# Transposing new token blocks by transfer instead of on TensorE, with re-sequenced engine programs, in a fused attention and feed-forward kernel

## The chip, the cores and the metric

The kernel runs on one core of a Trainium2 chip. The metric is the device time of one execution in microseconds (us). Before the change three executions took 2260.71 to 2260.99 us, with a median of 2260.98 us.

## The reference

The input x has 8 sequences of 1024 tokens with 256 channels, in f32. One block follows the other:

```python
x = x + layernorm(attention(layernorm(x)))
x = x + layernorm(ffn(layernorm(x)))

# attention: 16 heads of width 64, causal, with a bias by clipped distance
q, k, v = einsum('btc,hcd->bhtd', x, Wq), ...
scores = q @ k.T / sqrt(64) + rel_table[clip(rel + 16, 0, 32)]
out = softmax(causal(scores)) @ v            # heads side by side
return out @ Wp + bp

# ffn: x_prev is x shifted by one token
xr, xk = mu_r * x + (1 - mu_r) * x_prev, mu_k * x + (1 - mu_k) * x_prev
return sigmoid(xr @ W_r.T) * (square(relu(xk @ W_k.T)) @ W_v.T)
```

## The kernel before

**Tiling.** The work is cut into 64 units, one for each sequence and pair of heads (8 sequences, 8 pairs). One step n of the main sequence is nearly the same program for all n: it does the attention of unit n, the q, k and v projections of unit n + 2, and the tail (output projection, residual, feed-forward) of one block of 128 tokens. There are 64 blocks, so one step also brings in one new block. Products that need more than f16 are made of f16 high and low parts, with three matmuls for one: high by high, low by high, high by low.

**The new block.** In step n, block g = n + 10 is brought in. SyncE loads its 128x256 f32 rows into `xh` (`load_head`). VectorE takes mean and variance and makes the reciprocal root in eight small operations (`statistics`, `root_step`). GpSimd normalises `xh` in place (`head`, through `normalise`, line 376). TensorE transposes it as two 128x128 f32 transposes into a bank of PSUM called `misc` (`head_transpose`, line 549), ScalarE casts the bank to the f16 high part in the ring `xT` (`head_high`, line 885), and VectorE subtracts that from the bank to give the low part (`head_low`, line 1161). `xT` holds 16 blocks, two sequences. The projections (`project_qk`, line 563, and `project_v`, line 578) read `xT`. The first 8 blocks are made before the main sequence in the same way. There are 56 blocks made inside it, in steps -2 to 53.

**Score tiles.** Unit n has 12 score tiles, S0 to S11, of 512, 384, 256, 128, then five of 512, and 384, 256, 128 keys by queries for each of two heads (`score`, lines 607 and 611). They use two PSUM buffers in turn. S0 of the next unit is made at the end of a step. VectorE adds the bias where there is one (`add_bias`, line 1213), ScalarE exponentiates (`exponential`, line 926) and casts to the f16 high part (`high_probs`, line 944), GpSimd makes the low part (`low_probs`, line 1659; of S0 it is VectorE, line 1181). For S1 to S11 the exponential goes into one of two f32 copies in SBUF, and waits until GpSimd has finished the tile two before it.

**Row maxima.** Nine fills, F0 to F8, of one PSUM buffer (`fill`, lines 629 and 638) give rough scores. VectorE reduces each (`maxima`, lines 1192 and 1197), and TensorE transposes the maxima twice in a step (`transpose_maxima`, line 649, called mt0 and mt1). ScalarE writes the shift (`shift`, line 908), and SyncE spreads it over partitions (`load_shift`).

**Other tasks on TensorE.** q0, q1, k0, k1, v0, v1 are the projections in halves. o0 to o3 weigh the values (`weigh_values`, lines 672 to 674), o2 and o3 a step late. x2t, proj, rk and ffn belong to the tail. All of these write into two banks of `misc`. `TASKS` lists them in their order with a bank for each, and `opened` makes a task wait until the bank's previous task has been read. `project_qk` of q0 waits for `xt_lo`, the low part of the newest block of the ring.

**Order.** Each engine's program is written out by hand as one long list of calls. There is no dynamic scheduling: an instruction that waits holds up everything behind it on its engine. In a step TensorE goes: ffn, S1, F0, q0, o2, S2, S3, F1, o3, F2, q1, S4, F3, S5, k0, mt0, v0, F4, o0, S6, S7, F5, x2t, proj, S8, F6, S9, v1, o1, S10, F7, S11, rk, F8, S0 of the next unit, the head transposes, k1, mt1. Score tiles and fills use 64 rows of the array for each head, all others use 128.

Of the kernel before, what the change touches and what calls it, by code (L numbers as in the profile page):

```python
# [48 lines left out]
TASKS = [("ffn", 1, "ffn"), ("q0", 1, "qkv"), ("o2", 0, "prev"), ("o3", 0, "prev"), ("q1", 1, "qkv"),  # L49
         ("k0", 0, "qkv"), ("v0", 1, "qkv"), ("o0", 0, "att"), ("x2t", 0, "mix"), ("proj", 1, "proj"),  # L50
         ("v1", 0, "qkv"), ("o1", 1, "att"), ("rk", 1, "mix"), ("xt", 1, "xt"), ("k1", 0, "qkv")]
BANK = {name: bank for name, bank, _ in TASKS}
PART = {name: part for name, _, part in TASKS}
NAMES = [name for name, _, _ in TASKS]

# [66 lines left out]
def finished(name, n):  # L122

    return n + {"o2": 0, "o3": 0, "o0": 1, "o1": 1, "mt0": 2, "mt1": 2, "xt": HEAD_LEAD + 1, "proj": 1 - PROJ_LAG, "x2t": 1 - MIX_LAG, "rk": 1 - MIX_LAG,
                "ffn": 1 - FFN_LAG}.get(name, LEAD + 1)
# [17 lines left out]
def build(nc, x, wqkv, wp, bp, table, w_r, w_k, w_v, mu_r, mu_k, out):  # L143
    with ExitStack() as ctx:
# [45 lines left out]
        xh = sb("xh", [P, C], F32)  # L190
        xT = sb("xT", [P, 2, KT, RING], F16)
# [92 lines left out]

        full = {name: sem(f"full_{name}") for name in NAMES + ["mt0", "mt1"]}

        xh_in, xh_ready, xt_hi, xt_lo = sem("xh_in"), sem("xh_ready"), sem("xt_hi"), sem("xt_lo")
        proj_hi, proj_lo, v_hi, v_ready = sem("proj_hi"), sem("proj_lo"), sem("v_hi"), sem("v_ready")
# [52 lines left out]
        def freed(name, n):  # L341

            k = finished(name, n)
            if name[0] == "o" and name[1] in "0123":
                return o_ready[int(name[1])], k
            if name[0] in "qk":
                return proj_lo, 4 * k - 3 + ("q0", "q1", "k0", "k1").index(name) if name != "rk" else k
            if name in ("v0", "v1"):
                return v_ready, 2 * k - 1 + int(name[1])
            if name == "x2t":  # L350
                return mixed_ready, 2 * KT * k
            return {"proj": y_ready, "ffn": z_ready, "xt": xt_lo,
                    "rk": relu_ready}[name], k
# [34 lines left out]
        def _(sp):  # L388
# [92 lines left out]
            for span in ALL_SPANS:  # L481
                def body(m, par, at, has=span.has):
                    n = 2 * m + par
                    if has["xt"] and (not isinstance(m, int) or n > -LEAD):
                        load_head(n + HEAD_LEAD)
                    if has["att"]:
                        load_shift(m, par, 0, 1)
                    if has["next"] and par == 0:
                        load_values(m, par)
                    if has["proj"]:  # L490
                        load_outputs(n, par, at)
                    if has["next"]:
                        load_shift(m, par, 1, 0)
                    if has["proj"]:
                        load_residual(n - PROJ_LAG)
                    if has["next"] and par == 1:
                        load_values(m, par)
                    if has["prev"]:
                        store_chunk(m, par, 1, 1, at)
                    if has["att"]:  # L500
                        store_chunk(m, par, 0, 0, at)
                    if has["ffn"]:
                        store_out(n - FFN_LAG)
                rolled(sp, span, body)
# [23 lines left out]
        def _(pe):  # L528
# [189 lines left out]
            for span in ALL_SPANS:  # L718
                def body(m, par, at, span=span, has=span.has):
# [3 lines left out]
                    if has["ffn"]:  # L723
                        tail_value(n, span)
                    if has["att"]:
                        score(m, par, 0, 1, at)
                    if has["next"]:
# [3 lines left out]
                        fill(m, par, 0, at)  # L731
                    if has["qkv"]:
                        project_qk("q0", n, pair * P, ring, span)
                    if has["prev"]:
                        weigh_values(2, m, par, 1, span)
                    if has["att"]:
                        score(m, par, 0, 2, at)
                        score(m, par, 0, 3, at)
                    if has["next"]:
                        fill(m, par, 1, at)  # L740
                    if has["prev"]:
                        weigh_values(3, m, par, 1, span)
                    if has["next"]:
                        fill(m, par, 2, at)
                    if has["qkv"]:
                        project_qk("q1", n, pair * P, ring, span)
                    if has["att"]:
                        score(m, par, 0, 4, at)
                    if has["next"]:
                        fill(m, par, 3, at)  # L750
                    if has["att"]:
                        score(m, par, 0, 5, at)
                    if has["qkv"]:
                        project_qk("k0", n, pair * P, ring, span)
                    if has["next"]:
                        transpose_maxima(0, n)
                    if has["qkv"]:
                        project_v("v0", n, 4 * par, pair // 2 * 2 * P, ring, span)
                    if has["next"]:
                        fill(m, par, 4, at)  # L760
                    if has["att"]:
                        weigh_values(0, m, par, 0, span)
                        score(m, par, 0, 6, at)
                        score(m, par, 0, 7, at)
                    if has["next"]:
                        fill(m, par, 5, at)
                    if has["mix"]:
# [6 lines left out]
                    if has["att"]:  # L774
                        score(m, par, 0, 8, at)
                    if has["next"]:
                        fill(m, par, 6, at)
                    if has["att"]:
                        score(m, par, 0, 9, at)
                    if has["qkv"]:  # L780
                        project_v("v1", n, 4 * par + 2, pair // 2 * 2 * P, ring, span)
                    if has["att"]:
                        weigh_values(1, m, par, 0, span)
                        score(m, par, 0, 10, at)
                    if has["next"]:
                        fill(m, par, 7, at)
                    if has["att"]:
                        score(m, par, 0, 11, at)
                    if has["mix"]:
                        tail_gate_and_key(n, span)  # L790
# [3 lines left out]
                    if has["xt"]:  # L794
                        head_transpose(n, span)
                    if has["qkv"]:
                        project_qk("k1", n, pair * P, ring, span)
# [40 lines left out]
            tail_value(N, LAST)  # L838
            weigh_values(2, N // 2, 0, 1, LAST)
            weigh_values(3, N // 2, 0, 1, LAST)  # L840
            for j in range(NB):
# [32 lines left out]
        def _(act):  # L874
# [104 lines left out]
            for span in ALL_SPANS:  # L979
                def body(m, par, at, has=span.has):  # L980
# [6 lines left out]
                    if has["att"]:  # L987
                        exponential(m, par, 0, 1)
                        high_probs(m, par, 0, 1)
                    if has["qkv"]:  # L990
                        high_part("q0", m, par, at)
                    if has["att"]:
                        exponential(m, par, 0, 2)
                        high_probs(m, par, 0, 2)
                        exponential(m, par, 0, 3)
                    if has["qkv"]:
                        high_part("q1", m, par, at)
                    if has["att"]:
                        exponential(m, par, 0, 4)
                        high_probs(m, par, 0, 3)  # L1000
                        high_probs(m, par, 0, 4)
                    if has["qkv"]:
                        high_part("k0", m, par, at)
                    if has["next"]:
                        shift(m, par, 1, 0)
                    if has["att"]:
                        exponential(m, par, 0, 5)
                    if has["prev"]:
                        high_outputs(1, m, par, 1)
                    if has["qkv"]:  # L1010
                        values_high("v0", m, par)
                    if has["att"]:
                        high_probs(m, par, 0, 5)
                        exponential(m, par, 0, 6)
                    if has["mix"]:
                        tail_tokens(n)
                    if has["att"]:
                        high_probs(m, par, 0, 6)
                        exponential(m, par, 0, 7)
                        high_probs(m, par, 0, 7)  # L1020
                        exponential(m, par, 0, 8)
                        high_probs(m, par, 0, 8)
                        exponential(m, par, 0, 9)
                        high_probs(m, par, 0, 9)
                    if has["qkv"]:
                        values_high("v1", m, par)
                    if has["att"]:
                        exponential(m, par, 0, 10)
                        high_outputs(0, m, par, 0)
                    if has["mix"]:  # L1030
                        tail_gate(n)
                    if has["att"]:
                        high_probs(m, par, 0, 10)
                    if has["xt"]:
                        col = (m + HEAD_LEAD // 2) % (RING // P // 2) * 2 * P
                        col = (col if isinstance(m, int) else act.snap(col)) + par * P
                        head_high(n + HEAD_LEAD, col, misc[BANK["xt"]])
                    if has["att"]:
                        exponential(m, par, 0, 11)
                    if has["qkv"]:  # L1040
                        high_part("k1", m, par, at)
                    if has["next"]:
                        shift(m, par, 1, 1)
                        exponential(m, par, 1, 0)
                    if has["att"]:
# [754 lines left out]
```

## Time and profile before

| what | value |
|---|---|
| time, median of 3 | 2260.98 us |
| profiled execution, its own time | 2259.63 us |
| span of its instructions | 2257.8 us |
| TensorE matmul busy | 2133.1 us (94%) |
| VectorE busy | 1953.9 us (87%) |
| ScalarE busy | 1679.4 us (74%) |
| GpSimd busy | 1645.2 us (73%) |
| mean granted TensorE clock | 0.991 |
| chain that ended last | PE 86%, DVE 5%, ACT 3% |
| DMA queue of the kernel, share of 16 engines | 24.1% |

Busy time is summed over the whole span, the start and the end of the program included. The matmul ends are modelled. The chain that ended last is followed back from the last instruction to whatever released each step, and names where the time went. The profiled execution is 1.35 us shorter than the median.

### The profile page before, as it was taken

Reading aid. Unit: us, or ns where it says so; the run is one execution under the profiler, and the core shown is the slowest. Engines: PE = TensorE matmul, PEld = TensorE weight load, DVE = VectorE, ACT = ScalarE, POOL = GpSimd, SP = SyncE. Lnnn points to the kernel's source line nnn. Section 1 sums busy time; section 2 is a strip of 40 time slices with the busy share of each in tenths; the row PEclk is TensorE's granted clock in tenths of the full one; section 3 lists DMA queues with packets and bytes.
Section 4 is the critical chain, followed back from the end, with each engine's and each line's share of the span. In section 5 each row is a group of like instructions: output and inputs, shape, how many; then the busy total and the mean of one; then the engine's idle time right before and its main releaser. Section 6 shows DMA issues by size and latency. Waiting matters only on the chain.

```text
span 2257.8 us, 74896 instructions
## 1 busy us (share of the span) xinstructions
PE 2133.1 (94%) x29568; PEld 1456.7 (65%) x29568; DVE 1953.9 (87%) x5265; ACT 1679.4 (74%) x2526; POOL 1645.2 (73%) x1314
## 2 busy tenths in 40 slices
PE   3787899999999999999999999999999999999975
PEld 1354556676666767666666766666676667666664
DVE  6776778999999999999999999999999998888856
ACT  2576877787778777877877787787778778777733
POOL 1365766787778778777877877787787777777851
PEclk9999999999999999999999999999999999999998
DMA  7011012222321232232122223212322321222250
GB/s 176 23 39 44 28 37 60 68 60 61 72 61 49 63 71 62 58 73 67 42 63 73 62 56 72 70 44 58 72 62 57 73 67 49 48 66 65 58 125 22
DMA packets 306319, 139.77 MB, mean 62 GB/s; under 512 B 142512, under 2 KB 305200, under 8 KB 305968
## 3 DMA queue, kind: packets, MB, share of 16 engines
q1 hardware_dynamic: 305968, 134.98, 24.1%
q8 instruction: 234, 3.83, 0.7%
q14 instruction: 117, 0.96, 0.1%
HBM read 24.25 MB, written 43.06 MB: 30 GB/s over the span
## 4 chain that ended last, share of the span: by engine, by line
PE 86%; DVE 5%; ACT 3%; issue 2%; POOL 2%; DMA 1%; DVEq 0%; POOLq 0%; ACTq 0%; SPq 0%
PE score_ps L607 17%; PE misc L563 15%; PE misc L578 7%; PE misc L680 7%; PE misc L672 6%; PE max_ps L629 6%; PE misc L673 6%; PE misc L674 6%; PE score_ps L611 5%; PE misc L700 3%; PE misc L703 2%; PE max_ps L638 2%; PE misc L711 2%; POOL probs L1659 1%; ACT probs_f L926 1%
## 5 line engine op out<-in xcount | busy, mean ns | idle before, releaser
L1659 POOL TENSOR_TENSOR probs<-probs_f,probs 128x1024 f16<-128x1024 f32 (+3 forms) x704 | 1119.3, 1602 | 402.1 <-ACT probs L944 395.1
L926 ACT ACTIVATE probs_f<-score_ps,score_unit 128x1024 f32<-128x1024 f32 (+3 forms) x704 | 618.1, 878 | 271.4 <-DVE score_ps L1213 215.0
L1197 DVE TENSOR_REDUCE row_max<-max_ps 128x2 f32<-128x1024 f32 (+2 forms) x640 | 633.8, 1007 | 55.7 <-PE max_ps L638 53.7
L944 ACT CAST probs<-probs_f 128x1024 f16<-128x1024 f32 (+3 forms) x704 | 563.5, 810 | 10.5
L672 PE MATMUL misc<-v_pair,probs 128*128 128x65 f16 x4608 | 443.8, 193 | 2.2 <-DVE o_norm L1225 2.1
L673 PE MATMUL misc<-v_pair,probs 128*128 128x64 f16 x4608 | 442.8, 193 | 0.0
L674 PE MATMUL misc<-v_pair,probs 128*128 128x65 f16 x4608 | 441.7, 193 | 0.0
L672 PEld LDWEIGHTS misc<-v_pair,probs 128*128 128x128 f16 x4608 | 416.7, 97 | 23.3 <-issue 4.0
L673 PEld LDWEIGHTS misc<-v_pair,probs 128*128 128x128 f16 x4608 | 418.1, 97 | 8.0
L674 PEld LDWEIGHTS misc<-v_pair,probs 128*128 128x128 f16 x4608 | 418.3, 97 | 0.0
L563 PE MATMUL misc<-xT,w_split 128*128 128x512 f16 x1536 | 383.2, 386 | 10.7 <-DVE w_split L1316 6.7
L607 PE MATMUL score_ps<-q_hi,k_hi 64*128 64x512 f16 (+3 forms) x1536 | 254.9, 329 | 27.6 <-ACT probs_f L926 20.1
L1213 DVE TENSOR_TENSOR score_ps<-score_ps,bandT 128x288 f32<-128x288 f32 (+2 forms) x576 | 243.6, 423 | 25.3 <-PE score_ps L611 23.9
L563 PEld LDWEIGHTS misc<-xT,w_split 128*128 128x128 f16 x1536 | 135.5, 99 | 179.8 <-issue 50.5
L611 PE MATMUL score_ps<-shift_all,shift_unit 64*128 64x512 f16 (+3 forms) x1536 | 250.8, 323 | 0.0
L607 PE MATMUL score_ps<-q_lo,k_hi 64*128 64x512 f16 (+3 forms) x1536 | 250.7, 323 | 0.0
L607 PE MATMUL score_ps<-q_hi,k_lo 64*128 64x512 f16 (+3 forms) x1536 | 250.7, 323 | 0.0
L629 PE MATMUL max_ps<-k_hi,q_hi 64*128 64x512 f16 (+3 forms) x1536 | 221.7, 326 | 23.6 <-DVE row_max L1197 15.0
L578 PE MATMUL misc<-w_split,xT 128*128 128x256 f16 x1536 | 189.6, 273 | 0.0
L578 PEld LDWEIGHTS misc<-w_split,xT 128*128 128x128 f16 x1536 | 145.5, 98 | 40.6 <-issue 20.3
L680 PE MATMUL misc<-wp_split,oT 128*128 128x256 f16 x1344 | 157.1, 274 | 0.0
L607 PEld LDWEIGHTS score_ps<-q_hi,k_hi 64*128 64x128 f16 x1536 | 74.6, 93 | 115.3 <-issue 49.4
(168 smaller groups left out, 3715.2 us busy)
## 6 DMA issues: line engine op xcount, KB each, us to landing
v_pair<-v_calc SPq DMA_DIRECT2D x64, 516.0 KB, 4.0
o_scratch<-o_stage SPq DMA_DIRECT2D x128, 256.0 KB, 2.5
xh<-x SPq DMA_DIRECT2D x56, 128.0 KB, 2.5
x_res<-x SPq DMA_DIRECT2D x56, 128.0 KB, 2.1
out<-out_sb SPq DMA_DIRECT2D x56, 128.0 KB, 2.4
shift_all<-shift_row SPq DMA_DIRECT2D x256, 1.0 KB
probs<-wqkv SPq DMA_DIRECT2D x1, 3072.0 KB, 13.4
probs<-band_scratch SPq DMA_DIRECT2D x8, 144.0 KB, 3.8
```

Of the source, the lines that this page charges most:

```text
L563: last = pe.matmul(bank[:], w_split[:, w, which, k, bass.ds(pair, P)], xT[:, a, k, bass.ds(ring + half * 512, 512)], start=step == 0, stop ...
L578: last = pe.matmul(bank[:, i * 2 * P:(i + 1) * 2 * P], xT[:, a, k, bass.ds(ring + (first + i) * P, P)], w_split[:, w, 2, k, bass.ds(pairs, ...
L607: pe.matmul(tile[:, h, 0:width], k_part[rows, ring, keys], q_part[rows, ring, cols], start=step == 0, stop=False)
L611: last = pe.matmul(tile[:, h, 0:width], shift_unit[rows, :], shift_all[side][rows, cols], start=False, stop=True)
L629: last = pe.matmul(max_ps[:, h, col:col + width], qk_hi[0][rows, ring, i * P:(i + 1) * P], qk_hi[1][rows, ring, key:key + width], start=Tr ...
L672: pe.matmul(bank[:, at:at + D + 1], high, v_high, start=j == 0, stop=False)
L673: pe.matmul(bank[:, at:at + D], high, v_low, start=False, stop=False)
L674: last = pe.matmul(bank[:, at:at + D + 1], low, v_high, start=False, stop=j == i)
L926: nc.scalar.activation(dst, score_ps[t % 2][:, :, 0:width], ACT.Exp, scale=score_unit[:]).then_inc(exp_done, 1)
L944: nc.scalar.copy(dst, src).then_inc(hi_done, 1)
L1197: last = dve.tensor_reduce(dst[:, :, i % 4:i % 4 + 1], max_ps[:, :, col:col + width], AX.X, ALU.max)
L1659: pool.tensor_tensor(low, copy_of(par + ahead, t)[:, 0:2 * width], high, ALU.subtract).then_inc(lo_done_pool, 1)
```

## The change

The new block no longer goes through TensorE and PSUM. GpSimd normalises `xh` as before. ScalarE casts `xh` to f16 into half of a new buffer `x_parts` (`head_parts`), GpSimd subtracts to fill the other half (`head_low`), and SyncE issues one transposing transfer from `x_parts` into the ring (`transpose_head`). q0 waits for that transfer.

```diff
+        x_parts = sb("x_parts", [P, 2, C], F16)
...
             def load_head(g):
-                held(full["xt"], g)
+                held(x_lo, g - NB)
                 sp.dma_start(xh[:], x_rows[g]).then_inc(xh_in, 16)
+
+            def transpose_head(n):
+                g = n + HEAD_LEAD
+                held(x_lo, g - NB + 1)
+                held(full[LAST_PROJECTION], n + LEAD)
+                col = g % (RING // P) * P
+                sp.dma_start_transpose(xT[:].rearrange("p a k t -> p (a k) t")[:, :, col:col + P],
+                                       x_parts[:].rearrange("p a c -> p (a c)")).then_inc(xT_in, 16)
...
-            def head_transpose(n, span):
-                pe.wait_ge(xh_ready, n + LEAD + 1)
-                bank = opened("xt", n, span)
-                for k in range(KT):
-                    last = pe.transpose(bank[:, k * P:(k + 1) * P], xh[:, k * P:(k + 1) * P], ident[:])
-                last.then_inc(full["xt"], 1)
...
                 if name == "q0":
-                    pe.wait_ge(xt_lo, n + HEAD_LEAD if span.has["xt"] else G)
+                    pe.wait_ge(xt_lo, NB)
+                    wait(pe, xT_in, 16 * min(n + LEAD, G - NB))
...
+            def head_parts(n):
+                k = n + LEAD
+                act.wait_ge(xh_ready, k + 1)
+                wait(act, xT_in, 16 * k)
+                nc.scalar.copy(x_parts[:, 0, :], xh[:]).then_inc(x_hi, 1)
...
-                normalise(pool, "xh", xh[:], xh[:], k, (full["xt"], 0))
+                normalise(pool, "xh", xh[:], xh[:], k, (x_hi, 0))
+
+            def head_low(n):
+                pool.wait_ge(x_hi, n + LEAD + 1)
+                pool.tensor_tensor(x_parts[:, 1, :], xh[:], x_parts[:, 0, :], ALU.subtract).then_inc(x_lo, 1)
```

`head_high` and `head_low` of the old kind stay for the first 8 blocks alone.

All engines get new orders in the main sequence, and `TASKS` new banks to match:

- TensorE: S1, F0, o2, o3, S2, F1, S3, q0, ffn, F2, S4, S5, F3, o0, q1, v0, mt0, S6, F4, S7, o1, S8, F5, k0, k1, F6, v1, S9, S10, F7, x2t, proj, S11, F8, S0 of the next unit, rk, mt1.
- ScalarE (E exponential, H high part, by tile): E1, H1, E2, high parts of the previous second output half, q0, H2, E3, H3, E4, H4, E5, H5, shift for mt0, q1, E6, v0, H6, E7, H7, k0, E8, k1, H8, v1, high parts of the first output half, copy after x2t, E9, H9, E10, E11, H10, H11, shift for mt1, three gate operations after rk, E0 and H0 of the next unit, `head_parts`.
- GpSimd: low parts of tiles 1 to 4, low parts of the second output half of the previous unit, tiles 5 to 7, the residual normalisation, tiles 8 and 9, low parts of the first output half, tiles 10 and 11, `head`, `final` (two operations), `head_low`, `residual` (two operations).
- SyncE: shift for the columns of S4 to S11, `load_head`, values, shift for the next unit, outputs (a transposing transfer of four times the size), residual, store of outputs, values, store of outputs, store of the result, `transpose_head`.
- VectorE: `gated` and the outputs 2 and 3 change places, roots and maxima are spread anew, and the old `head_low` is gone. The operations are otherwise the same.

## Rows read from the trace of the kernel before

**Rows 1.** Windows view: busy time of each engine in two stretches.

```profile
60.00:352.00 292.00, 249.90 (x3542) 152.41 (x3543) 218.53 (x428) 211.16 (x301) 172.10 (x116) 0.98 0.15 39
352.00:1857.00 1505.00, 1503.46 (x21208) 1038.75 (x21206) 1383.12 (x3830) 1185.44 (x1787) 1199.61 (x958) 1.00 0.25 62
```

**Rows 2.** Timeline of TensorE, end of a step (start, duration, instruction).

```profile
1449.19 0.39 PE L629 MATMUL max_ps<-k_hi,q_hi 64*128 64x512 f16 x2
...
1449.51 0.38 PE L607 MATMUL score_ps<-q_hi,k_hi 64*128 64x512 f16 x2
...
1450.47 0.44 PE L549 MATMUL misc<-ident,xh 128*128 128x128 f32 x2
1450.74 1.46 PE L563 MATMUL misc<-xT,w_split 128*128 128x512 f16 x6
...
1452.15 1.03 PE L711 MATMUL misc<-wv_sb,k_act 128*128 128x256 f32 x4
```

**Rows 3.** Timeline of TensorE, the beginning of a step.

```profile
1420.29 0.34 PE L607 MATMUL score_ps<-q_hi,k_hi 64*128 64x384 f16 x2
...
1421.36 1.47 PE L563 MATMUL misc<-xT,w_split 128*128 128x512 f16 x6
1422.66 0.19 PE L672 MATMUL misc<-v_pair,probs 128*128 128x65 f16 x1
...
1424.74 0.28 PE L607 MATMUL score_ps<-q_hi,k_hi 64*128 64x256 f16 x2
...
1425.83 0.20 PE L672 MATMUL misc<-v_pair,probs 128*128 128x65 f16 x1
...
1428.64 0.39 PE L629 MATMUL max_ps<-k_hi,q_hi 64*128 64x128 f16 x4
...
1429.06 1.47 PE L563 MATMUL misc<-xT,w_split 128*128 128x512 f16 x6
1430.46 0.39 PE L607 MATMUL score_ps<-q_hi,k_hi 64*128 64x512 f16 x2
```

**Rows 4.** Timeline of TensorE, tail tasks of one step.

```profile
1438.65 0.44 PE L693 MATMUL misc<-ident,y 128*128 128x128 f32 x2
...
1441.64 0.39 PE L607 MATMUL score_ps<-q_hi,k_hi 64*128 64x512 f16 x2
...
1447.23 1.13 PE L700 MATMUL misc<-wr_sb,mixed 128*128 128x256 f32 x4
```

**Rows 5.** Timeline of ScalarE in the same step.

```profile
1439.12 0.37 ACT L958 COPY x2T<-misc 128x256 f32<-128x256 f32 x1 [0.23 <-PE misc L693]
...
1445.32 0.90 ACT L926 ACTIVATE probs_f<-score_ps,score_unit 128x768 f32<-128x768 f32 x1
1446.25 0.83 ACT L944 CAST probs<-probs_f 128x768 f16<-128x768 f32 x1
...
1449.29 0.39 ACT L965 ACTIVATE gate<-misc 128x256 f32<-128x256 f32 x1 [0.38 <-PE misc L703]
...
1450.31 0.60 ACT L944 CAST probs<-probs_f 128x512 f16<-128x512 f32 x1
```

**Rows 6.** Timeline of GpSimd in the same step.

```profile
1422.36 2.28 POOL L1665 TENSOR_TENSOR o_stage<-o_norm,o_stage 128x512 f16<-128x512 f32 x2
...
1433.03 0.67 POOL L1659 TENSOR_TENSOR probs<-probs_f,probs 128x256 f16<-128x256 f32 x1 [3.65 <-ACT probs L944]
...
1448.80 1.64 POOL L1659 TENSOR_TENSOR probs<-probs_f,probs 128x768 f16<-128x768 f32 x1
1451.45 1.22 POOL L376 TENSOR_SCALAR out_sb<-z,z_mv,z_r 128x256 f32<-128x256 f32 x1 [1.01 <-DVE z_r L1143]
1452.76 0.72 POOL L1692 TENSOR_TENSOR out_sb<-x,out_sb 128x256 f32<-128x256 f32 x1
```

**Rows 7.** SyncE's timeline, and the DMA view of that issue (us to landing).

```profile
1427.62 2.33 SPq L429 DMA_TRANSPOSE oT<-o_scratch  x1
...
oT<-o_scratch SPq DMA_TRANSPOSE x1, 4.4
```

More of the change, by code:

```diff
@@ L54 @@
 NAMES = [name for name, _, _ in TASKS]
+LAST_PROJECTION = [name for name in NAMES if name in ("q0", "q1", "k0", "k1", "v0", "v1")][-1]
 WP_SPLIT = 5
@@ L122, in finished @@
 def finished(name, n):
-    return n + {"o2": 0, "o3": 0, "o0": 1, "o1": 1, "mt0": 2, "mt1": 2, "xt": HEAD_LEAD + 1, "proj": 1 - PROJ_LAG, "x2t": 1 - MIX_LAG, "rk": 1 - MIX_LAG,
+    return n + {"o2": 0, "o3": 0, "o0": 1, "o1": 1, "mt0": 2, "mt1": 2, "proj": 1 - PROJ_LAG, "x2t": 1 - MIX_LAG, "rk": 1 - MIX_LAG,
                 "ffn": 1 - FFN_LAG}.get(name, LEAD + 1)
@@ L283, in build @@
             sem("x0_in"), sem("x0_stats"), sem("x0_aggr"), sem("x0_root"), sem("x0_ready"))
-        full = {name: sem(f"full_{name}") for name in NAMES + ["mt0", "mt1"]}
+        full = {name: sem(f"full_{name}") for name in NAMES + ["xt", "mt0", "mt1"]}
         xh_in, xh_ready, xt_hi, xt_lo = sem("xh_in"), sem("xh_ready"), sem("xt_hi"), sem("xt_lo")
+        x_hi, x_lo, xT_in = sem("x_hi"), sem("x_lo"), sem("xT_in")
         proj_hi, proj_lo, v_hi, v_ready = sem("proj_hi"), sem("proj_lo"), sem("v_hi"), sem("v_ready")
@@ L483, in body @@
                     n = 2 * m + par
+                    if has["att"]:
+                        load_shift(m, par, 0, 1)
                     if has["xt"] and (not isinstance(m, int) or n > -LEAD):
                         load_head(n + HEAD_LEAD)
-                    if has["att"]:
-                        load_shift(m, par, 0, 1)
                     if has["next"] and par == 0:
                         load_values(m, par)
-                    if has["proj"]:
-                        load_outputs(n, par, at)
                     if has["next"]:
@@ L503, in body @@
                         store_out(n - FFN_LAG)
+                    if has["xt"]:
+                        transpose_head(n)
                 rolled(sp, span, body)
@@ L731, in body @@
                         fill(m, par, 0, at)
+                    if has["prev"]:
+                        weigh_values(2, m, par, 1, span)
+                        weigh_values(3, m, par, 1, span)
+                    if has["att"]:
+                        score(m, par, 0, 2, at)
+                    if has["next"]:
+                        fill(m, par, 1, at)
+                    if has["att"]:
+                        score(m, par, 0, 3, at)
                     if has["qkv"]:
                         project_qk("q0", n, pair * P, ring, span)
[L734 to L742, printed above, removed]
+                    if has["ffn"]:
+                        tail_value(n, span)
                     if has["next"]:
                         fill(m, par, 2, at)
-                    if has["qkv"]:
-                        project_qk("q1", n, pair * P, ring, span)
                     if has["att"]:
                         score(m, par, 0, 4, at)
+                        score(m, par, 0, 5, at)
                     if has["next"]:
@@ L761, in body @@
                     if has["att"]:
-                        weigh_values(0, m, par, 0, span)
-                        score(m, par, 0, 6, at)
                         score(m, par, 0, 7, at)
+                        weigh_values(1, m, par, 0, span)
+                        score(m, par, 0, 8, at)
                     if has["next"]:
                         fill(m, par, 5, at)
+                    if has["qkv"]:
+                        project_qk("k0", n, pair * P, ring, span)
+                        project_qk("k1", n, pair * P, ring, span)
+                    if has["next"]:
+                        fill(m, par, 6, at)
+                    if has["qkv"]:
+                        project_v("v1", n, 4 * par + 2, pair // 2 * 2 * P, ring, span)
+                    if has["att"]:
+                        score(m, par, 0, 9, at)
+                        score(m, par, 0, 10, at)
+                    if has["next"]:
+                        fill(m, par, 7, at)
                     if has["mix"]:
@@ L793, in body @@
                         score(m, par, 1, 0, at)
[L794 to L797, printed above, removed]
+                    if has["mix"]:
+                        tail_gate_and_key(n, span)
                     if has["next"]:
@@ L989, in body @@
                         high_probs(m, par, 0, 1)
+                        exponential(m, par, 0, 2)
+                    if has["prev"]:
+                        high_outputs(1, m, par, 1)
                     if has["qkv"]:
@@ L992, in body @@
                     if has["att"]:
-                        exponential(m, par, 0, 2)
                         high_probs(m, par, 0, 2)
                         exponential(m, par, 0, 3)
+                        high_probs(m, par, 0, 3)
+                        exponential(m, par, 0, 4)
+                        high_probs(m, par, 0, 4)
+                        exponential(m, par, 0, 5)
+                        high_probs(m, par, 0, 5)
+                    if has["next"]:
+                        shift(m, par, 1, 0)
                     if has["qkv"]:
@@ L998, in body @@
                     if has["att"]:
[L999 to L1009, printed above, removed]
+                        exponential(m, par, 0, 6)
                     if has["qkv"]:
                         values_high("v0", m, par)
[L1012 to L1016, printed above, removed]
                     if has["att"]:
@@ L1479, in body @@
+                    if has["qkv"]:
+                        low_part("k1", m, par, at)
+                        values_low("v1", m, par)
+                    if has["att"]:
+                        add_bias(m, par, 0, 9, at)
+                    if has["next"]:
+                        maxima(m, par, 1, 7)
+                    if has["att"]:
+                        add_bias(m, par, 0, 10, at)
                     if has["mix"]:
                         mix(n)
+                    if has["att"]:
+                        add_bias(m, par, 0, 11, at)
@@ L1481, in body @@
+                    if has["next"]:
+                        maxima(m, par, 1, 8)
+                    if has["proj"]:
+                        projected(n)
+                    if has["next"]:
+                        join_maxima(m, par, 1)
+                    if has["proj"]:
+                        statistics("y", y, n - PROJ_LAG, y_ready, n - PROJ_LAG + 1)
                     if has["ffn"]:
                         root_step("z", n - FFN_LAG, 4)
-                    if has["xt"]:
-                        root_step("xh", n + LEAD, 4)
@@ L1537, in body @@
                     if has["proj"]:
+                        root_step("y", n - PROJ_LAG, 3)
+                    if has["ffn"]:
+                        root_step("z", n - FFN_LAG, 5)
+                    if has["proj"]:
+                        root_step("y", n - PROJ_LAG, 4)
+                    if has["ffn"]:
+                        root_step("z", n - FFN_LAG, 6)
+                    if has["proj"]:
+                        root_step("y", n - PROJ_LAG, 5)
                         root_step("y", n - PROJ_LAG, 6)
-                    if has["qkv"]:
-                        low_part("k1", m, par, at)
+                    if has["ffn"]:
+                        root_step("z", n - FFN_LAG, 7)
                     if has["proj"]:
@@ L1723, in body @@
                         low_probs(m, par, 0, 4)
-                    if has["mix"]:
-                        residual_norm(n, par)
+                    if has["prev"]:
+                        low_outputs(1, m, par, 1)
                     if has["att"]:
```

236 lines of the change are left out of this document (95 added, 141 removed).

## The prediction, made before the result was known

> **What bounds the kernel now.** First the windows view: in the stretch of full steps, 352 to 1857 us, TensorE is busy 1503.46 of 1505 us, at full clock, while VectorE has 92%, ScalarE 79% and GpSimd 80% [rows 1]. The reader should see that no other engine costs anything there: TensorE's own issue time is the whole time. The stretch holds 46 steps, so a step takes 1505 / 46 = 32.72 us. From 60 to 352 us it is busy only 249.9 of 292 us [rows 1]. There the steps have no tail work yet, and other engines hold it up in places. Second, TensorE's timeline, where the distance from one start to the next is what a task really costs (durations overlap) [rows 2 to 4]. Third, the timelines of ScalarE, GpSimd and SyncE, for the new chain that the change makes [rows 5 to 7].
>
> **What goes from TensorE.** The two head transposes start at 1450.47, and k1 at 1450.74: 0.27 us a step [rows 2]. Behind them goes VectorE's subtraction, hidden today by TensorE's saturation, worth nothing as long as TensorE bounds. ScalarE's cast keeps its size.
>
> **What the new order on TensorE saves.** Each change between tasks on 64 rows and on 128 rows costs time. A fill inside a 64-row group takes 1449.51 - 1449.19 = 0.32 us [rows 2], and a fill between 128-row tasks takes 0.42 (1428.64 to 1429.06) [rows 3], so 0.10 going to 128 rows. A projection followed by 128-row work takes 1.30 (1421.36 to 1422.66), followed by a score tile 1.40 (1429.06 to 1430.46) [rows 3], so 0.10 going back. The old step has nine 64-row groups, the new one eight (S1 F0; S2 F1 S3; F2 S4 S5 F3; S6 F4 S7; S8 F5; F6; S9 S10 F7; S11 F8 S0). That saves 0.20 us a step. In steps without tail work the counts are equal. So with nothing late, a full step is 0.27 + 0.20 = 0.47 us shorter.
>
> **What the change adds: a wait at q0.** In step n, q0 waits for the transfer issued by the program of step n - 1, though its data is needed at most once in eight steps. I lay both sides out from the start of S1.
>
> q0's place on TensorE: S1, F0 and the change to 128 rows 1.07; o2 2.08 - 0.10 = 1.98, as o3 follows it; o3 with the change back 2.81; S2, F1, S3 with a change 1.09 (the same three in the old order, 1424.74 to 1425.83) [rows 3]. Together 6.95 us.
>
> The transfer's chain starts at x2t of the step before. From there to S1: x2t and proj 2.99 [rows 4]; S11, a quarter of a 512 tile, where S0 with its change is 0.96, so 0.22; F8 and S0 with a change 1.28 [rows 2]; rk, 1447.23 to 1449.19, 1.96 less the change 0.10, so 1.86 [rows 2, 4]; mt1 0.11 (k1 and mt1 take 1.41 together, k1 1.30) and a change 0.10 [rows 2, 3]. Sum 6.56, so x2t starts at -6.56. ScalarE copies it 0.47 later (1438.65 to 1439.12), and can start E9 about 0.27 after that; H9 starts 0.93 after E9 and lasts 0.83 [rows 4, 5]. GpSimd can start tile 9 at -4.03. From there it works without a gap: tile 9 1.64, output low parts 2.28 / 2 = 1.14, tile 10 about 1.12 and tile 11 0.67, `head` about 1.2, the first half of `final` 1.31 up to its second half, which lasts 0.72, then `head_low` about 0.67, as the low part of a tile with 256 elements [rows 6]. Sum 8.5, so `head_low` ends at 4.45 and SyncE issues at about 4.55. ScalarE's side must end by 3.8 and does so within 0.3: shift about 0.3, gate operations 1.02, E0 and H0 at most 4/3 of 0.90 and 0.83, the copy 0.4, about 4 us in all [rows 5].
>
> The landing is not in the trace. The nearest row is the transposing transfer of outputs: four times the size, issued in 2.33 us, landed at 4.4 [rows 7]. If issue time goes with size, the new one is issued in 0.58 and lands at 4.4 - 1.75 = 2.65. From below I take 2.0, as if only the part of that time outside the issue counted (4.4 - 2.33 = 2.07); from above 4.4, if a transfer of any size costs what this one does. I take 2.65, as both are the same kind of instruction. Then q0 may start at 4.55 + 2.65 = 7.2 and finds its place at 6.95: a wait of 0.25, and with 0.1 us for the semaphores 0.35 us a step. Nothing makes this up, as all later work on TensorE moves with q0 and the chain hangs on x2t of the same step. At 2.07 there is no wait, at 4.4 it is 2.1 us.
>
> The Trainium skill, in "DMA: Bandwidth & Descriptors" (section on the anatomy of one DMA), gives a fixed 2.0 us plus bytes over 436 GB/s, for a GpSimd-issued transfer. An estimate from it for 128 KB is 2.3 us, which would make the wait about 0.1 and a full step 0.4 us shorter. The larger transfer would take 3.2 by that rule, and the trace has 4.4 [rows 7], so the rule does not agree there.
>
> **What else moves.** SyncE: the next `load_shift` now stands behind the store of the result and `transpose_head`. It is issued at about 4.55 + 0.6 and could land by 8.5, and S4 starts at 9.6. Cover 1 us; a full-size issue of 2.33 would use it up. VectorE: 30.1 us of work in a step of 32.3, less the subtraction, is the tightest engine [rows 1]. Going through its list beside TensorE's, the near places are q1's low part before o1 (about 0.4 us), k0's before v1 (0.3) and v1's before proj (0.3). I cost them at nothing; one late by 0.3 would cost 0.3 a step. GpSimd gets 0.67 us a step and goes from 26.1 to 26.8 of 32.3 [rows 1, 6].
>
> **The sum.** Full steps with a new block: 45 x (0.35 - 0.47) = -5.4. Eight more without one: 8 x -0.20 = -1.6. Steps before 352 us: TensorE idles 42 us there [rows 1], part of it at set-up that stays. The old order runs tiles 5 to 8 back to back against GpSimd's pace, and the new one spreads them. I put 1 us a step for 8 steps, after paying the same wait, so -8, with bounds of -16 and +8. Set-up and end: nothing, within 3 us. Together -15: 2259.63 - 15 = 2244.6 for the profiled execution's own time, and 1.35 more against the median: **2246 us**. This kernel's measurement can tell about 0.2% (4.5 us) from no change.
>
> **The rivals.**
> - *The transfer is hidden* (landing 2.1 or less, or GpSimd earlier than I add up). The wait is 0: 45 x -0.47 = -21, with the rest -10: 2229. For it: the 4.4 us of the large one includes an issue that a small one may not need. Against: 0.35 us would have to go from a chain whose terms are nearly all measured, or from the landing. Chance 0.24.
> - *The wait grows to a new bound, slower* (the other side). A transfer read from SBUF in pieces costs more to issue than one from DRAM. From a landing of 3.0 the wait is 0.7, the steps' loss 45 x 0.23 = 10 eats the gain elsewhere, and beyond it the time is above before. At 4.4: 45 x (2.1 - 0.47) = 73, and the early steps pay as well: 2335. Its middle is a landing of 3.5, wait 1.2, +33 and little from the early steps: 2290. For it: the store of the result is in the queue 0.6 us ahead, and all 16 engines' packets must land. Against: the clean row at 4.4 for four times the bytes. Chance 0.22. The Trainium skill, same page (section on why a DMA increments its semaphore by 16), describes SBUF-to-SBUF transposes on earlier generations as one push command per tile, and has a lower price for a DRAM source; no transpose from SBUF is in this trace.
> - *VectorE's handoffs come late.* With the forecast's wait and 0.3 us more: +13 on the forecast, 2260, no change. For it: 92% busy with in-order waits. Against: q0's wait gives VectorE room. Chance 0.12.
> - *The change doesn't do what it says*: the transposes stay elsewhere on TensorE. The diff leaves none. Chance 0.
>
> **How the numbers follow.** The forecast has 0.42, and its own range is 2238 to 2256. The rivals have 0.24, 0.22 and 0.12. Faster by over 0.2% takes the forecast, the hidden case: 0.66 less 0.03 for the forecast's upper end, so 0.63. Within 0.2%: the VectorE case and that end, 0.13. Slower: 0.24. The range goes from 2226, just under the hidden case, to 2282, which leaves the worse half of the slow case out.
>
> **What would show it.** TensorE has no L549 row, and eight 64-row groups. q0's L563 waits for the DMA xT once in each step, with a mean near 0.35. The transfer's row has an issue near 0.6 and a landing near 2.65. `head_low` ends about 4.5 us after S1. A full step is near 32.6 us. I am wrong if q0 waits over 0.7, or if TensorE waits elsewhere in each step, for VectorE's `q_lo`, `k_lo` or `row_max`.

## The result, and the profile after

| | before | after |
|---|---|---|
| median of the runs | 2260.98 us | 2325.01 us (2322.42 to 2329.78, 4 runs) |
| ratio, 95% interval | 1 | 1.0282 [1.0268, 1.0295] |
| span of the profiled execution | 2257.8 us | 2320.6 us |

The change makes the kernel 64 us slower (2325.01 - 2260.98). The prediction was 2246 us, faster, with a range up to 2282; the result lies outside it.

The windows view of after, with the stretches of [rows 1] (from:to and length, then busy us and count of TensorE's matmuls, its weight loads, VectorE, ScalarE and GpSimd, the granted clock, the DMA engines' busy share and GB/s):

```profile
60.00:352.00 292.00, 245.02 (x3486) 149.08 (x3486) 210.47 (x411) 207.62 (x296) 176.84 (x123) 0.95 0.15 41
352.00:1857.00 1505.00, 1441.92 (x20308) 983.88 (x20309) 1325.91 (x3638) 1147.84 (x1723) 1179.94 (x966) 0.99 0.27 64
```

TensorE was busy for 1503.46 of 1505 us before [rows 1] and is for 1441.92 now: it idles 63 us, and no other engine does more than before. The waits view of TensorE, from 352 to 1857 us (line, what it waited for: us in total, times, longest):

```profile
PE misc L569 <- issue: 61.0, 43, 2.7
PE max_ps L655 <- DVE row_max L1207: 0.9, 1, 0.9
PE score_ps L613 <- ACT probs_f L933: 0.6, 2, 0.3
PE misc L569 <- DMA xT<-x_parts: 0.5, 1, 0.5
```

Nearly all the idle time, 61.5 of 63 us, stands before one line, L569, the projections from the ring (L563 before), once in each of 44 steps. The view says "issue" for 43 of them. The timeline says what it was. TensorE, from S1 to the task behind q0 (start, duration, instruction, idle time before it):

```profile
1427.56 0.34 PE L613 MATMUL score_ps<-q_hi,k_hi 64*128 64x384 f16 x2
...
1428.63 0.20 PE L678 MATMUL misc<-v_pair,probs 128*128 128x65 f16 x1
...
1433.42 0.28 PE L613 MATMUL score_ps<-q_hi,k_hi 64*128 64x256 f16 x2
...
1434.36 0.22 PE L617 MATMUL score_ps<-shift_all,shift_unit 64*128 64x128 f16 x2
...
1435.38 1.46 PE L569 MATMUL misc<-xT,w_split 128*128 128x512 f16 x6 [0.81 <-issue]
1436.67 1.03 PE L717 MATMUL misc<-wv_sb,k_act 128*128 128x256 f32 x4
```

SyncE in the same step, and the tile view's row of the transfer (duration of the issue: min/median/max in ns):

```profile
1432.19 0.34 SPq L455 DMA_DIRECT2D out<-out_sb  x1
1432.85 1.24 SPq L450 DMA_TRANSPOSE xT<-x_parts  x1
1434.19 1.29 SPq L402 DMA_DIRECT2D shift_all<-shift_row  x2
...
L450 SPq DMA_TRANSPOSE xT<-x_parts x56: 1203/1238/2421, 55.1 to 1914.6; - x56
```

q0 was ready at 1435.38 - 0.81 = 1434.57, 7.01 us after S1. The transfer is issued at 1432.85, 5.29 us after S1, and lands 2.4 us later, at about 1435.25; q0 starts about 0.1 us after that. In a later step the transfer takes 4.1 us, lands at about 1499.65 + 4.1 = 1503.75, and q0 starts at 1503.88, again about 0.1 us behind it:

```profile
1499.65 1.22 SPq L450 DMA_TRANSPOSE xT<-x_parts  x1
```

```profile
1503.88 2.44 PE L569 MATMUL misc<-xT,w_split 128*128 128x512 f16 x6 [2.50 <-issue]
1506.11 1.77 PE L717 MATMUL misc<-wv_sb,k_act 128*128 128x256 f32 x4
```

So the wait is for the landing, whatever the view calls it. The second pair of rows shows one thing more. From q0 to the ffn task takes 1506.11 - 1503.88 = 2.23 us, where it took 1436.67 - 1435.38 = 1.29 in the other step. The windows view over another such step (a wait of 2.0 us, then q0 at 449.4), and over the step with the short wait:

```profile
449.40:453.40 4.00, 3.95 (x12) 2.00 (x12) 0.13 (x1) 1.19 (x3) 0.01 (x1) 0.57 0.11 33
...
1435.00:1439.00 4.00, 3.62 (x28) 2.03 (x30) 2.77 (x6) 2.65 (x6) 2.27 (x2) 1.00 0.50 144
```

The granted clock is 0.57 on average behind the long wait and 1.00 behind the short one: the engine ran mostly at 1.2 GHz, the lower level, where otherwise it has 2.4. That costs another 1.7 us in such a step: the step with the wait of 2.50 us takes 36.53 us, where one with a wait of 0.81 takes 33.18, and of the 3.35 us between them the longer wait is 1.69.

The length of each step, from the start of the exponential of S0 to the next one on ScalarE's timeline, gives an account that all the runs below share. In the tables, steps 9 to 53 are the 45 with tail work and a new block, steps 54 to 61 have tail work and no new block (step 54 still waits at q0, for the last one).

### The profile page after: what moved, and what is told of

The parts are those of the page before. It is cut to its first block and busy times, and to the rows that moved or that the text cites. A ratio compares the mean times of both kernels' runs of the same rounds, so it can differ in the third digit from the quotient of the medians.

```text
span 2320.6 us, 74837 instructions
## 1 busy us (share of the span) xinstructions
PE 2125.9 (92%) x29456; PEld 1438.6 (62%) x29456; DVE 1945.4 (84%) x5209; ACT 1684.9 (73%) x2526; POOL 1681.5 (72%) x1370
## 5 line engine op out<-in xcount | busy, mean ns | idle before, releaser
L569 PE MATMUL misc<-xT,w_split 128*128 128x512 f16 x1536 | 374.0, 387 | 84.5 <-issue 71.8
L678 PE MATMUL misc<-v_pair,probs 128*128 128x65 f16 x4608 | 438.4, 194 | 0.6 <-issue 0.6
L679 PE MATMUL misc<-v_pair,probs 128*128 128x64 f16 x4608 | 436.7, 193 | 0.0
L680 PE MATMUL misc<-v_pair,probs 128*128 128x65 f16 x4608 | 435.8, 193 | 0.0
L569 PEld LDWEIGHTS misc<-xT,w_split 128*128 128x128 f16 x1536 | 137.8, 99 | 242.0 <-issue 102.5
L881 ACT CAST q_hi<-misc 128x512 f16<-128x512 f32 x128 | 73.1, 571 | 108.4 <-PE misc L569 108.4
```

The lines of the kernel that those rows point to most:

```text
L569: last = pe.matmul(bank[:], w_split[:, w, which, k, bass.ds(pair, P)], xT[:, a, k, bass.ds(ring + half * 512, 512)], start=step == 0, stop ...
L678: pe.matmul(bank[:, at:at + D + 1], high, v_high, start=j == 0, stop=False)
L679: pe.matmul(bank[:, at:at + D], high, v_low, start=False, stop=False)
L680: last = pe.matmul(bank[:, at:at + D + 1], low, v_high, start=False, stop=j == i)
```

## The experiments

**What was asked.** The theory: q0 waits for the landing, which is both issued later and takes longer than forecast, and the rest of the new order gives what it should. The rivals: the new order itself costs time, VectorE's handoffs are late, or the idle time has nothing to do with the slower clock. Four kernels were run first, and e5_roots and e6_warm after their results. The kernel before was run again beside each group (2261.9 us beside the first four, 2264.06 beside the last two), and the ratios are to these.

### e1_relax: q0 waits for a transfer of an earlier step

```diff
-                    wait(pe, xT_in, 16 * min(n + LEAD, G - NB))
+                    wait(pe, xT_in, 16 * ((n + LEAD) // NB * NB))
```

The wait is then for what q0 really reads, and only once in NB steps for the transfer just issued. Everything else stays.

> q0 waits for the new block only where the projections first read it, in one step of eight; the transfer, its chain and every engine's order stay. If the wait at q0 is what made the changed kernel slow, it is left in 7 of 56 steps, a full step takes 32.35 us as the steps without a new block do, and the time falls from 2325 by about 70 to about 2253 us. If the new orders on VectorE, ScalarE or GpSimd are the true limit, another wait takes its place on TensorE in each step, and the time stays above 2290.

Measured: 2251.03 us, ratio 0.9958 to before [0.9943, 0.9972]. TensorE's waits from 376 to 1930 us:

```profile
PE misc L569 <- issue: 8.4, 6, 2.7
PE score_ps L613 <- DMA shift_all<-shift_row: 2.2, 7, 0.5
```

One wait's threshold holds 74 us of the time, the slower clock included, and turns the change from slower to faster, by 0.4%. The second row is a cover of the prediction that was used up: S4 waits for the shift that stands behind the transposing transfer in SyncE's queue, in 7 steps, by 2.2 us in all.

### e2_early: the same wait, the transfer issued earlier

The edit puts `head_low` ahead of `final` on GpSimd, `head_parts` ahead of E0's cast on ScalarE, and the transfer ahead of the store on SyncE.

```diff
@@ GpSimd
                         head(n)
+                        head_low(n)
                     if has["ffn"]:
                         final(n, par)
-                    if has["xt"]:
-                        head_low(n)
@@ ScalarE
-                        high_probs(m, par, 1, 0)
                     if has["xt"]:
                         head_parts(n)
+                    if has["next"]:
+                        high_probs(m, par, 1, 0)
@@ SyncE
-                    if has["ffn"]:
-                        store_out(n - FFN_LAG)
                     if has["xt"]:
                         transpose_head(n)
+                    if has["ffn"]:
+                        store_out(n - FFN_LAG)
```

> The wait at q0 stays in every step, but the chain before it is shortened: GpSimd makes the low part before the final normalisation, ScalarE makes the high part before the cast of S0, SyncE issues the transfer before the store of the result. The issue should move from 5.3 to about 3.7 us after S1. With landings of 2.4 to 4.3 us the wait should then be 0 in most steps and at most 1.1, and the time about 2257. If landing gets longer because the transfer now meets other work, or GpSimd's delayed low parts hold up the exponentials, it stays above 2290.

Measured: 2253.53 us (8 runs), ratio 0.9963 [0.9952, 0.9974]. The transfer goes out 3.64 us after S1 instead of 5.29. What is left of the waits, from 352 to 1857 us, and GpSimd's wait for ScalarE's copy, which keeps the issue from coming earlier still:

```profile
PE misc L569 <- issue: 10.2, 15, 1.2
```

```profile
1421.02 0.68 POOL L1672 TENSOR_TENSOR x_parts<-xh,x_parts 128x256 f16<-128x256 f32 x1 [1.00 <-ACT x_parts L893]
```

The wait can go either way: by asking for less, or by having the data sooner. The remaining 15 waits are those of the 15 longest landings, 3.5 to 4.5 us.

### e3_both: e1 and e2 together

> Both edits. With the wait theory nothing is left to wait for at q0, so the time is that of full steps of 32.35 us: about 2247 us, below the kernel before (2261). A rival, that the reordered GpSimd costs more than the wait did in the one step of eight, puts it above the run with the relaxed wait alone.

Measured: 2238.62 us (2236.16 to 2241.2), ratio 0.9902 [0.9887, 0.9917]: faster than both kernels, 22 us below before and 86 below after. The windows view of the full steps:

```profile
400.00:1800.00 1400.00, 1398.67 (x19863) 960.48 (x19859) 1301.50 (x3586) 1117.93 (x1688) 1159.66 (x950) 1.00 0.28 67
```

TensorE is full again (1398.67 of 1400 us). With 1.3 us of waits left at q0 in two steps, the new order shows what it gives. The step lengths (us, sums over steps; a full step is 32.82 before with a new block):

| steps | before | after | e1_relax | e2_early | e3_both | e4_later | e5_roots | e6_warm |
|---|---|---|---|---|---|---|---|---|
| 1 to 8 | 259.5 | 266.2 | 262.1 | 266.2 | 262.2 | 266.6 | 265.3 | 266.2 |
| 9 to 53 | 1476.5 | 1533.9 | 1468.8 | 1465.1 | 1456.2 | 1568.1 | 1513.0 | 1525.4 |

In e3_both nearly every step of the second row has 32.34 us (45 x 32.34 = 1455.3). The 1476.5 of before less 1456.2 is 20.3, or 0.45 us a step, against the 0.47 of the prediction. The forecast of 2247 for this kernel was 8 us too high: its steps of 32.35 us came, and it does not say what it took for the rest.

### e4_later: the same transfer, issued behind the next shift

```diff
                         load_shift(m, par, 0, 1)
+                    if runs("xt", n - 1):
+                        transpose_head(n - 1)
...
-                    if has["xt"]:
-                        transpose_head(n)
```

> The transfer is issued behind the next shift's two transfers, 1.3 us later; nothing else moves. If only the wait counts, each of some 54 steps loses 1.3 us and the time is about 2395. If the granted clock also falls after each wait of 2 us or more, as it seems to in a quarter of the steps now, nearly all steps lose a further 1.7 us, and the time is about 2450 to 2490.

Measured: 2358.14 us (one run), 33 above after. TensorE's waits from 400 to 1880 us:

```profile
PE misc L569 <- issue: 88.4, 42, 3.0
```

88.4 / 42 = 2.1 us on average, where after has 61.0 / 43 = 1.4. Both forecasts were too high. Most steps take 34.33, which is 32.34 + 2.0, and eleven take 36 to 37, with the slower clock again: it fell behind only 11 of the 39 waits of 1.94 us and more, so a long wait alone does not decide it. The issue comes 1.1 us later (5.1 us after the start of E0 instead of 4.0, means over the steps), but the mean wait is only 0.7 longer, because the landings became shorter: their mean fell from 3.0 to 2.6 us, their median from 2.9 to 2.4. The transfer issued later also took a different time to land; see the last section.

### e5_roots: VectorE's last root steps for z moved up

In after, GpSimd waits for VectorE's root of z before the output task that stands ahead of `head_low`. GpSimd in the step of the first timeline:

```profile
1428.16 1.21 POOL L378 TENSOR_SCALAR xh<-xh,xh_mv,xh_r 128x256 f32<-128x256 f32 x1
1430.04 1.22 POOL L378 TENSOR_SCALAR out_sb<-z,z_mv,z_r 128x256 f32<-128x256 f32 x1 [0.67 <-DVE z_r L1146]
1431.35 0.73 POOL L1693 TENSOR_TENSOR out_sb<-x,out_sb 128x256 f32<-128x256 f32 x1
1432.04 0.68 POOL L1671 TENSOR_TENSOR x_parts<-xh,x_parts 128x256 f16<-128x256 f32 x1
```

The edit moves steps 4 to 7 of `root_step("z", ...)` in VectorE's list each to an earlier place; the first of the four:

```diff
                         root_step("xh", n + LEAD, 6)
+                    if has["ffn"]:
+                        root_step("z", n - FFN_LAG, 4)
```

> The changed kernel with VectorE's last four root steps of z moved up among the maxima, so that GpSimd's final normalisation no longer waits 0.67 us for them; nothing else moves. If the chain before the transfer sets the wait at q0, the issue comes 0.6 to 0.7 us earlier, the mean wait goes from 1.44 to about 0.8 us, fewer waits are long enough for the clock to fall, and the time goes from 2325 to about 2285. If VectorE's order has no slack for it, or the landing alone makes the wait, it stays within 10 us of 2325.

Measured: 2299.47 us (2293.77 to 2302.75), ratio 1.0153 [1.0132, 1.0174]. SyncE's row of the transfer in the step whose S1 starts at 1419.77:

```profile
1424.50 1.23 SPq L450 DMA_TRANSPOSE xT<-x_parts  x1
```

It goes out 4.73 us after S1, 0.56 earlier than in after, and over the steps 0.6 earlier in the mean. The gain is 26 us of the 40 expected. In the profiled executions it is 23: TensorE's waits at q0 fall from 64 to 49 us in all, and the clock falls in four steps instead of eight, 7 us at 1.7 each. The mean wait is 1.1 us and not the 0.8 that was expected, because the mean landing was 3.2 us instead of 3.0. So an earlier issue shortens the wait, though not by its whole 0.6 us here.

### e6_warm: TensorE works during the wait

Six matmuls on columns already in the ring are put ahead of q0's wait. Their results are overwritten by q0; nothing is left out.

```diff
+                    if span.has["xt"] and n >= FFN_LAG:
+                        pe.wait_ge(o_ready[3], n)
+                        for _ in range(6):
+                            pe.matmul(misc[BANK[name]][:], w_split[:, 0, which, 0, bass.ds(pair, P)],
+                                      xT[:, 0, 0, bass.ds(ring, 512)], start=True, stop=True)
```

> The changed kernel with six more matmuls, of 512 columns, ahead of q0's wait in the steps with a tail, so that TensorE works 1.3 us of its wait; they read columns of the ring that are there already, and their result is overwritten by q0. The transfer's chain stays. If the idle time itself is what lowers the granted clock, no stretch behind q0 runs below full clock any more: 8 steps gain 1.75 us each (-14), and the steps that waited less than 1.3 us lose up to 0.5 each (+8), so about 2319 with no step over 35.2 us. If the clock falls for another reason, steps of 36 us stay and the time is about 2333.

Measured: 2317.17 us (2316.28 to 2322.74), ratio 1.024 [1.0225, 1.0256], 8 below after. The windows view of the full steps:

```profile
400.00:1900.00 1500.00, 1489.94 (x20575) 1005.97 (x20575) 1331.56 (x3663) 1146.49 (x1725) 1183.78 (x972) 1.00 0.27 64
```

The granted clock is 1.00, where the full steps of after have 0.99, with eight stretches at the lower level. None of steps 9 to 53 is longer than 35.04 us; after has eight between 36.0 and 36.6. Step 54, which gets no extra matmuls but still waits (2.4 us), takes 36.44, with the slower clock. The six matmuls also cost something: they take about 6 x 0.22 = 1.3 us, more than the 0.8 us for which the short waits last, and a step with a short wait goes from 33.18 to 33.63 us. More work on the engine made the kernel faster: with no idle time before q0 above 1.2 us, the clock did not fall in any of the 45 steps, so it was this idle time that lowered it in after.

## Why the prediction was wrong, step by step

- **What bounds the kernel**: right for the full steps. The waits at q0, the clock behind them and the saving on TensorE add up to the change of steps 9 to 53 (see the account below). The prediction's step of 32.72 counts 46 steps in a stretch that holds 45.9; a step of before takes 32.82.
- **The transposes gone and one 64-row group fewer, 0.47 us a step**: right. 0.45 measured over 45 steps in e3_both; steps 55 to 61 take 32.34 us in after, where 32.56 to 32.69 stood before (forecast 0.20 less, measured 0.22 to 0.35).
- **q0's place, 6.95 us after S1**: right, 7.01.
- **The issue at 4.55 us after S1**: wrong by 0.74. The prediction says that GpSimd works "without a gap" from tile 9 on. The profile has a gap of 0.67 there, for VectorE's root of z. Before, GpSimd waited 1.01 us for this same value (the `z_r` row in [rows 6]); I used the row's duration and passed over the bracket behind it. The words "I cost them at nothing" were said of TensorE's handoffs from VectorE, and GpSimd's were not gone through.
- **The landing of 2.65 us**: the mean of the 45 is 3.00, so 0.35 too low. The clean landing is 2.4, below what I took. The Trainium skill, "DMA: Bandwidth & Descriptors" (section on the anatomy of one DMA), gives 2.0 us plus bytes over 436 GB/s, for a transfer issued by GpSimd. By it an estimate for this one, which SyncE issues, is 2.3 us; the trace's clean 2.4 is within 0.1 us of it, and the stretched ones, 2.8 to 4.3, are not. The assumption that the issue time goes with size was wrong as well: 1.24 us for a quarter of the bytes that took 2.33 [rows 7], not 0.58. The two also differ in their source, SBUF here and DRAM there, and no run compares the sources at one size.
- **The wait at q0, 0.35 us a step**: this is the term that failed. It measured 63.7 us in the 45 steps, 1.41 a step, where 0.35 + 0.74 + 0.35 gives 1.44. Once q0's wait is above nothing, every error in its chain is paid in full, in each step. I had bounded the landing from 2.0 to 4.4, and the issue not at all.
- **The clock**: not in the prediction. Eight steps at 1.7 us, 14 us; e6_warm got 8.5 of them back (1533.9 - 1525.4), net of what its extra matmuls cost.
- **Cover of 1 us for S4's shift**: held in after, used up in e1_relax (2.2 us).
- **VectorE's handoffs to TensorE at nothing**: right. From 376 to 1930 us no row of after's waits names them.
- **The early steps, -8 us**: wrong, +6.7 in steps 1 to 8. In e1_relax and e3_both, where almost no wait at q0 is left, they are still 2.6 to 2.7 us longer than before, so the new order gains nothing there, and the q0 waits add 4. TensorE's largest wait from 110 to 370 us, before:

```profile
PE score_ps L607 <- ACT probs_f L926: 16.6, 16, 8.6
```

and in after:

```profile
PE score_ps L613 <- ACT probs_f L933: 28.0, 26, 9.8
...
PE misc L569 <- issue: 5.5, 6, 1.6
```

Score tiles wait for ScalarE's exponentials 26 times instead of 16, while waits for VectorE's maxima, 8.6 us before, are gone. What ScalarE's exponentials wait for in the same stretch, before:

```profile
ACT probs_f L926 <- POOL probs L1659: 16.0, 17, 12.7
ACT probs_f L926 <- DVE score_ps L1213: 15.0, 17, 1.5
```

and in after:

```profile
ACT probs_f L933 <- POOL probs L1656: 23.7, 23, 9.5
ACT probs_f L933 <- DVE score_ps L1216: 19.6, 16, 2.6
```

So the exponentials wait longer for GpSimd's low parts than before, and for VectorE's bias too. The guess that spreading the tiles helps against GpSimd looked at the right engine, but the wait for it became longer and not shorter. That the new order itself does this is what the rows suggest; no run takes the early steps' order by itself.
- **The chances**: by the prediction's own terms, "within 0.2%" comes to 0.12 + 0.03 = 0.15 and "slower" to 0.22, where it has 0.13 and 0.24. Nothing in the forecast hangs on it.

The account of the profiled executions, after less before (2320.6 - 2257.8 = 62.8 us): steps 9 to 53 give +57.4, as -21 (45 x 0.47) + 64 (waits) + 14 (clock); steps 1 to 8 give +6.7; the rest is -1. Against the forecast the miss is 79 us: 48 for the waits (45 x 1.06), 14 for the clock, 15 for the early steps, and 2 that are not accounted for.

**The rivals.** "The wait grows to a new bound" is what happened, at the place and by the mechanism named, with a chance of 0.22 and a price of 2290. It gave a landing of 3.5 with the issue on time; what came was a landing of 3.0 with the issue late, and the clock on top. Its point from which the change loses, a wait of 0.47 plus what the early steps give, is what e2_early shows from the other side: with a mean wait of 10.2 / 45 = 0.23 us the kernel is faster than before. The hidden transfer did not come, VectorE did not hold up TensorE in the full steps, and no transpose was left on TensorE there.

## What to carry to other kernels

When a change hangs the bounding engine on a chain through three others, go through each link's own waits in the profile, and ask for the slack: here a chain that fitted on paper to 0.3 us lost 1.4. A semaphore threshold that asks for the newest transfer, where the data of an older one is read, is paid in each step; the cheapest repair was one line (74 us). And where a wait at the bounding engine can't be avoided, add the slower clock behind it to its price, or give the engine something to do.

## What the runs showed of the hardware

**Landings come in two kinds.** Of 48 of these transfers in after (300 to 1930 us), 18 landed in 2.4 us, 4 in 2.5 to 2.6 and 26 in 2.8 to 4.3. The DMA view over 3 us from the issue, for the one at 1432.85 (2.4 us; DMA: busy share of the engines in 40 slices, then packets, MB and share by queue):

```profile
DMA  0039999620000000279999996310000000000000
q1 hardware_dynamic: 696, 0.26, 34.9%
```

and for the one at 1499.65 (4.1 us):

```profile
DMA  0169898400000000399999989990900000990000
q1 hardware_dynamic: 663, 0.26, 86.9%
q8 instruction: 1, 0.02, 2.9%
```

In the slow one a fetch of instructions, one packet of 16 KB, shares the DMA engines with the transfer. The count, for 48 transfers of each run, with a landing called fast up to 2.5 us and slow above, and a fetch counted that starts between 1.0 us before the issue and 2.3 us after it:

| run | slow, with a fetch | fast, with a fetch |
|---|---|---|
| after | 27 of 28 | 2 of 20 |
| e3_both | 29 of 29 | 9 of 19 |
| e4_later | 9 of 9 | 15 of 39 |

The one slow landing of after without a fetch took 2.6 us; the 26 of 2.8 us and more all had one. So in these runs a landing of 2.8 us and more always came with a fetch, and a fetch not always with a slow landing; e2_early and e5_roots have one landing each, of 4.4 and 4.5 us, with no fetch in that stretch. In e4_later a fetch that starts before the transfer seems to do little: of the 15 fast landings that had one, 13 had it more than 0.25 us before the issue. That would fit the shorter landings behind its later issue, which met a fetch later than that 11 times in 48, where after did 24 times. No run takes the fetches away, so this stays an association, not a shown cause.

**The clock fell behind waits of about 2 us.** In after it fell to the lower level behind eight of the thirteen waits at q0 of 1.94 us and more, and behind none of the shorter ones. Waits of 1.97, 2.03, 2.33, 2.56 and 2.70 us left it alone. In e4_later it fell behind 11 of the 39 waits of 1.94 us and more, in e5_roots behind three of the seven and once behind one of 1.86. No run has it fall in the full steps behind a wait shorter than that. e6_warm shows that the idle time is the cause in after; why it has no effect in some steps stays open.

**A small transposing transfer is not cheap to issue**: 1.24 us of SyncE for 128 KB in the median and up to 2.42, against 0.34 for the plain store next to it.
